# Attention block on one core: 12 of 72 probability units of a pass are turned by VectorE and transfers in place of TensorE

## The reference

```python
y = x * rsqrt(mean(x * x) + 1e-6) * rms_w           # x: 2 x 1024 x 512
q, k, v = split(y @ w_in.T)                          # 32 q heads, 8 k heads, 8 v heads, 64 wide
qk = rope(q) @ rope(k).T * 64 ** -0.5, causal
o = softmax(qk) @ v
x = layernorm(x + (x + o @ w_out.T))
x = layernorm(x + ternary(x) @ (ternary(weight) + variation).T)
```

## Time and profile before

| | |
|---|---|
| median of 3 runs | 1429.83 us (1427.52 to 1430.16) |
| the profiled execution | 1428.65 us, its span 1426.9 us |
| TensorE busy | 1355.1 us, 95% |
| VectorE busy | 1148.0 us, 80% |
| ScalarE busy | 1077.9 us, 76% |
| GpSimd busy | 872.0 us, 61% |
| granted TensorE clock | 0.988 of full |
| moved by transfers | 61.79 MB |

### The profile page before, as it was taken

How to read it: one execution, slowest core, us unless ns; L and a number is a source line. 1 busy time by engine, 2 the same in 40 slices (tenths; PEclk the granted TensorE clock), 3 DMA queues, 4 the chain that set the end, 5 groups by cost and what they waited for, 6 DMA issues and landing times.

```text
span 1426.9 us, 25073 instructions
## 1 busy us (share of the span) xinstructions
PE 1355.1 (95%) x7296; PEld 1112.1 (78%) x7296; DVE 1148.0 (80%) x3031; ACT 1077.9 (76%) x2277; POOL 872.0 (61%) x846
## 2 busy tenths in 40 slices
PE   4799999999999999999999999999999999997787
PEld 3678787888888888888888888888888888885565
DVE  5687777888787888888797888888797887876897
ACT  4768778787787878778787878778787878785553
POOL 1457467476646766376656766376646766477766
PEclk9799999999999999999999999999999999998999
DMA  6002101211101111111101111111101111111012
GB/s 206 20 19 60 49 26 28 54 30 45 35 24 49 55 29 31 50 34 46 34 24 49 55 29 31 44 40 45 34 24 49 51 33 31 29 37 51 31 46 77
DMA packets 45160, 61.79 MB, mean 43 GB/s; under 512 B 10464, under 2 KB 27104, under 8 KB 45024
## 3 DMA queue, kind: packets, MB, share of 16 engines
q1 hardware_dynamic: 45024, 60.20, 14.6%
HBM read 34.74 MB, written 4.46 MB: 27 GB/s over the span
## 4 chain that ended last, share of the span: by engine, by line
PE 74%; DVE 9%; ACT 6%; issue 4%; POOL 3%; DMA 3%; SPq 1%; DVEq 0%; POOLq 0%; ACTq 0%
PE s L1081 17%; PE x L1093 16%; PE t L1127 14%; PE x L1111 9%; PE ot L1052 8%; PE ot L1050 8%; DMA spread<-recip_rows 3%; DVE prob L949 2%; DVE prob_lo L1017 2%; ACT prob L781 2%; ACT prob_hi L752 1%; PE x L1101 1%; DVE win_lo L967 1%; DVE stats L843 1%; ACT q_t L816 1%
## 5 line engine op out<-in xcount | busy, mean ns | idle before, releaser
L752 ACT ACTIVATE prob_hi<-t 128x512 fp32r<-128x512 f32 x576 | 340.2, 594 | 150.7 <-PE t L1127 144.4
L1017 DVE TENSOR_TENSOR prob_lo<-t,prob_hi 128x512 fp32r<-128x512 f32 x576 | 394.4, 686 | 64.0 <-ACT prob_hi L752 58.1
L1081 PE MATMUL s<-k_t,q_t 128*128 128x512 f32 (+3 forms) x1536 | 411.1, 372 | 24.7 <-DVE neg_max L949 13.7
L781 ACT ACTIVATE prob<-prob,neg_max 128x896 f32<-128x896 f32 (+7 forms) x512 | 393.3, 770 | 36.6 <-DVE neg_max L949 35.1
L1127 PE MATMUL t<-ident,prob 128*128 128x128 f32 x2304 | 348.1, 274 | 2.8 <-ACT prob L781 2.7
L1127 PEld LDWEIGHTS t<-ident,prob 128*128 128x128 f32 x2304 | 288.7, 141 | 77.6 <-ACT prob L781 4.9
L949 DVE CUSTOM_DVE_ANT_0 prob<-s,mask 128x512 f32<-128x512 f32 (+3 forms) x512 | 292.3, 585 | 62.8 <-PE s L1081 38.9
L1081 PEld LDWEIGHTS s<-k_t,q_t 128*128 128x128 f32 x1536 | 246.0, 192 | 60.7 <-DVE neg_max L949 19.8
L725 POOL TENSOR_TENSOR o_lo<-o_raw,o_hi 128x256 fp32r<-128x256 f32 x128 | 95.0, 742 | 256.5 <-ACT o_hi L836 255.9
L1050 PE MATMUL ot<-prob_hi,v_sb 128*128 128x512 f32 x576 | 239.9, 416 | 3.8 <-DVE o_raw L999 3.0
L1052 PE MATMUL ot<-prob_lo,v_sb 128*128 128x512 f32 x576 | 232.8, 404 | 8.3 <-DVE prob_lo L1017 8.3
(11 more groups left out here) (88 smaller groups left out, 2051.7 us busy)
## 6 DMA issues: line engine op xcount, KB each, us to landing
swapped<-flat SPq DMA_DIRECT2D x320, 64.0 KB, 2.0
spread<-recip_rows SPq DMA_DIRECT2D x128, 128.0 KB
recip_rows<-turned SPq DMA_DIRECT2D x512, 0.5 KB
raw<-L_attn_w_in SPq DMA_DIRECT2D x8, 768.0 KB, 7.7
raw<-L_attn_w_out SPq DMA_DIRECT2D x8, 512.0 KB, 3.7
out<-acc SPq DMA_DIRECT2D x16, 256.0 KB, 2.0
acc<-L_attn_x SPq DMA_DIRECT2D x3, 1024.0 KB, 10.1
acc<-L_attn_x SPq DMA_DIRECT2D x4, 256.0 KB, 3.6
```

The source lines that it names most:

```text
L752: act.activation(prob_hi[:, u % 2, :], t_ps[u % 2][:, :], ACT.Copy).then_inc(prob_hi_done, 1)
L781: act.activation(row, row, ACT.Exp, bias=neg_max[:, kk % 4, h:h + 1], scale=-1.0, accum_out=total[:, kk % 4, h:h + 1]).then_inc(ex_done, 1)
L1017: dve.tensor_tensor(prob_lo[:, u % 2, :], t_ps[u % 2][:, :], prob_hi[:, u % 2, :].bitcast(F32), ALU.subtract).then_inc(prob_lo_done, 1)
L1081: mm = pe.matmul(s_ps[:, off:off + cols], q_t[:, h, s * P:(s + 1) * P], k_t[:, part, keys:keys + cols], start=(part == 0), stop=(part == 1))
```

## The change

Six units of each batch, (s, j) = (5,3), (6,3), (6,4), (7,3), (7,4), (7,5), twelve of 72 in a pass and 96 in the program, no longer go through TensorE's transposes and PSUM. Instead:

1. `bt` on VectorE: one transpose instruction, in place, turns the 16 pieces of 32x32 of the unit's 128x512 block.
2. `bt` on SP: one transfer of 256 KB takes the block to `block_rows` in memory (four slots).
3. `bm` on SP: four transfers of 64 KB bring it back, so that each piece lands on its own partitions.
4. ScalarE's `prob_hi` and VectorE's `prob_lo` read these units from `prob` in SBUF.

For this the rows are laid out anew, for all units: within a unit's 512 columns the head is the innermost index, so a head's consecutive keys lie four floats (16 bytes) apart. VectorE's score write, ScalarE's exponential (read and write) and TensorE's load of the block to be turned all use this step. A unit is now one slot of `prob`. `P_AFTER` and `P_BASE` stay. All tables of places are set anew, in all passes. The transposes of TensorE that stay are counted by `turns(u)`.

```diff
+BY_BLOCKS = ((5, 3), (6, 3), (6, 4), (7, 3), (7, 4), (7, 5))
+BLOCK_SLOTS = 4
...
+    for n, (made, moved) in enumerate(at_pass["BLOCKS"]):
+        put(made, ("bt", n))
+        put(moved, ("bm", n))
...
+        def blocks_before(u):
+            return sum(b * UNITS + first_unit(s) + j < u for b, s, j in map(block_unit, range(AWAY)))
+        def by_blocks(u):
+            return u < BODY and unit_of(u)[1:] in BY_BLOCKS
+        def turns(u):
+            passes, u = divmod(u, BODY)
+            return passes * (BODY - AWAY) + u - blocks_before(u)
...
-            start, cols = P_BASE[s] * BANK, (s + 1) * P
-            return prob[:, start + h * cols:start + (h + 1) * cols]
+            start, cols = (P_BASE[s] + 4 * c) * BANK, min(HALF, s + 1 - 4 * c) * BANK
+            return prob[:, start:start + cols].rearrange("p (k h) -> p h k", h=HG)[:, h]
...
SP:
+                        elif e[0] == "bt":
+                            wait(sp, blocks_done, g, AWAY, n + 1)
+                            wait(sp, blocks_in[some], g, 64 * ROUNDS, 64 * (n // BLOCK_SLOTS))
+                            sp.dma_start(block_d[some], prob_unit(*block_unit(n)[1:])).then_inc(blocks_out[some], 16)
+                        elif e[0] == "bm":
+                            wait(sp, blocks_out[some], g, 16 * ROUNDS, 16 * (n // BLOCK_SLOTS + 1))
+                            from_d = block_d[some].rearrange("(a j) (b f) -> b j a f", a=4, b=4)
+                            to = prob_unit(*block_unit(n)[1:]).rearrange("p (a f) -> p a f", a=4)
+                            for b in range(4):
+                                sp.dma_start(to[32 * b:32 * b + 32], from_d[b]).then_inc(blocks_in[some], 16)
ScalarE:
+                        if by_blocks(u):
+                            wait(act, blocks_in[n % BLOCK_SLOTS], g, 64 * ROUNDS, 64 * (n // BLOCK_SLOTS + 1))
+                            act.activation(hi.rearrange("p (h q) -> p h q", h=HG),
+                                           prob_unit(s, j).rearrange("p (q h) -> p h q", h=HG), ACT.Copy)
VectorE:
+                        elif e[0] == "bt":
+                            wait(dve, ex_done, g, 2 * NT * HG, (b * NT + s + 1) * HG)
+                            cells = prob_unit(s, j).rearrange("p (b i h) -> p b h i", b=4, h=HG)
+                            dve.transpose(cells, cells).then_inc(blocks_done, 1)
...
+                        if by_blocks(u):
+                            dve.tensor_tensor(lo, prob_unit(s, j).rearrange("p (q h) -> p h q", h=HG), hi, ALU.subtract)
TensorE:
+                        if not by_blocks(u):
+                            for h in range(HG):
+                                cells = prob_unit(s, j).rearrange("p (k h) -> p h k", h=HG)[:, h]
+                                mm = pe.transpose(t_ps[u % 2][:, h * P:(h + 1) * P], cells, ident[:, :])
```

More of the change, by code:

```diff
@@ L96 @@
     SCORES=(
[14 rows of a table removed]
[14 rows of a table added]
     ),
     PROJECT=(
[5 rows of a table removed]
[5 rows of a table added]
     ),
-    SQUARES=(0, 3),
+    SQUARES=(2, 39),
     NORMS=(
-        (20, 24), (26, 34), (36, 41), (42, 44), (49, 57), (65, 97), (107, 136), (151, 167)
+        (9, 21), (22, 27), (39, 46), (47, 56), (59, 62), (65, 113), (125, 143), (149, 160)
     ),
-    W_OUT=(10, 20),
-    LOAD=213,
-    W_IN=(296, 296, 300, 300),
+    W_OUT=(12, 38),
+    LOAD=221,
+    W_IN=(262, 263, 283, 284),
     OUTPUT=(
[3 rows of a table removed]
[3 rows of a table added]
+    ),
+    BLOCKS=(
+        (111, 128), (153, 175), (158, 178), (192, 227), (195, 240), (234, 240), (402, 409), (437, 454), (437, 468),
+        (508, 517), (510, 524), (511, 537)
     ))
@@ L133 @@
     SCORES=(
[14 rows of a table removed]
[14 rows of a table added]
     ),
     PROJECT=(
[4 rows of a table removed]
-    ),
-    W_OUT=(51, 51),
-    LOAD=177,
-    W_IN=(255, 260, 287, 294),
[4 rows of a table added]
+    ),
+    W_OUT=(49, 57),
+    LOAD=196,
+    W_IN=(261, 287, 297, 302),
     OUTPUT=(
[3 rows of a table removed]
[3 rows of a table added]
+    ),
+    BLOCKS=(
+        (113, 117), (150, 189), (155, 190), (200, 220), (203, 228), (218, 252), (402, 412), (445, 457), (456, 467),
+        (493, 523), (497, 524), (502, 526)
     ))
@@ L265, in first_plan, with seq_block @@
     return plan.number()
-def seq_block(nc, x, w_in, w_out, rms_w, ffn_w, ffn_r, cos, sin, ident_d, tri_d, row_d, out):
+def seq_block(nc, x, w_in, w_out, rms_w, ffn_w, ffn_r, cos, sin, ident_d, tri_d, row_d, block_d, out):
     B, S, D = x.shape
@@ L390, in seq_block @@
         t_done = sem("t_done")
+        blocks_done = sem("blocks_done")
+        blocks_out = [sem(f"blocks_out{n}") for n in range(BLOCK_SLOTS)]
+        blocks_in = [sem(f"blocks_in{n}") for n in range(BLOCK_SLOTS)]
         recip_done = sem("recip_done")
@@ L474, in unit_of, with block_unit @@
             return b, s, u - first_unit(s)
+        AWAY = 2 * len(BY_BLOCKS)
+        def block_unit(n):
+            b, n = divmod(n, len(BY_BLOCKS))
+            return b, *BY_BLOCKS[n]
+        def blocks_before(u):
[5 more added lines that the diff above has]
+            return passes * (BODY - AWAY) + u - blocks_before(u)
+        TURNS = BODY - AWAY
+        ROUNDS = AWAY // BLOCK_SLOTS
         def over_bodies(eng, one):
@@ L489, in xn_tile, with prob_row, prob_unit @@
             return scratch(9 + t % 3) if t < FIRST_TILES else raw[:, 2, :]
-        def prob_row(s, h):
-            start, cols = P_BASE[s] * BANK, (s + 1) * P
-            return prob[:, start + h * cols:start + (h + 1) * cols]
+        def prob_row(s, h, c):
+            start, cols = (P_BASE[s] + 4 * c) * BANK, min(HALF, s + 1 - 4 * c) * BANK
+            return prob[:, start:start + cols].rearrange("p (k h) -> p h k", h=HG)[:, h]
+        def prob_unit(s, j):
+            return prob[:, (P_BASE[s] + j) * BANK:(P_BASE[s] + j + 1) * BANK]
         def below(eng, t):
@@ L748, in one @@
                     if u < plan.units:
-                        wait(act, t_done, g, BODY, u + 1)
                         wait(act, pv_done, g, BODY, u - 1)
-                        act.activation(prob_hi[:, u % 2, :], t_ps[u % 2][:, :], ACT.Copy).then_inc(prob_hi_done, 1)
+                        hi = prob_hi[:, u % 2, :]
+                        if by_blocks(u):
+                            n, (_, s, j) = blocks_before(u), unit_of(u)
+                            wait(act, blocks_in[n % BLOCK_SLOTS], g, 64 * ROUNDS, 64 * (n // BLOCK_SLOTS + 1))
+                            act.activation(hi.rearrange("p (h q) -> p h q", h=HG),
+                                           prob_unit(s, j).rearrange("p (q h) -> p h q", h=HG), ACT.Copy
+                                           ).then_inc(prob_hi_done, 1)
+                        else:
+                            wait(act, t_done, g, TURNS, turns(u) + 1)
+                            act.activation(hi, t_ps[u % 2][:, :], ACT.Copy).then_inc(prob_hi_done, 1)
                     for e in plan.ahead[u] + plan.behind[u]:
@@ L776, in one @@
                             kk = b * NT + s
-                            row = prob_row(s, h)
                             wait(act, max_done, g, STEPS_MADE, scored(b, s, h, s // HALF) + 1)
                             wait(act, recip_done, g, 2 * NT, kk - 3)
+                            start = P_BASE[s] * BANK
+                            row = prob[:, start:start + (s + 1) * BANK].rearrange("p (k h) -> p h k", h=HG)[:, h]
                             act.activation(row, row, ACT.Exp, bias=neg_max[:, kk % 4, h:h + 1], scale=-1.0,
@@ L943, in events @@
                             back, last = P_AFTER[s]
-                            wait(dve, t_done, g, BODY, (b + back) * UNITS + first_unit(last + 1))
+                            wait(dve, t_done, g, TURNS, turns((b + back) * UNITS + first_unit(last + 1)))
                             wait(dve, sc_full, g, STEPS_MADE, n + 1)
@@ L948, in events @@
                                 wait(dve, max_done, g, STEPS_MADE, n - 1)
-                            dve.tensor_tensor_reduce(out=prob_row(s, h)[:, c * BANK:c * BANK + cols],
+                            dve.tensor_tensor_reduce(out=prob_row(s, h, c),
                                                      in0=s_ps[:, off:off + cols], in1=mask[:, seen:seen + cols],
@@ L1016, in one @@
                         wait(dve, pv_done, g, BODY, u - 1)
-                        dve.tensor_tensor(prob_lo[:, u % 2, :], t_ps[u % 2][:, :], prob_hi[:, u % 2, :].bitcast(F32),
-                                          ALU.subtract).then_inc(prob_lo_done, 1)
+                        hi, lo = prob_hi[:, u % 2, :].bitcast(F32), prob_lo[:, u % 2, :]
+                        if by_blocks(u):
+                            _, s, j = unit_of(u)
+                            hi, lo = [x.rearrange("p (h q) -> p h q", h=HG) for x in (hi, lo)]
+                            dve.tensor_tensor(lo, prob_unit(s, j).rearrange("p (q h) -> p h q", h=HG), hi, ALU.subtract
```

(14 more changed lines are left out.)

18 lines of the change are left out of this document (14 added, 4 removed), and 147 rows, old and new, of tables (FIRST, LAYER, OUTPUT, PROJECT).

## The result

The changed kernel takes 1791.93 us (median of 4 runs, 1791.05 to 1794.64), beside 1429.99 of the kernel before: a ratio of 1.254 (95% interval 1.2524 to 1.2554), 362 us more. The forecast of 1413 us is wrong, and the time lies beyond the range's upper end of 1600.

A forecast was written before the change was run, and what follows sets the result against it. TensorE was taken to bound the six middle passes. Seven passes at 5.3 - 2.5 us saved, rounded to -19.6, and +2.6 in the final pass gave -17 us: 1411.6, or 1413 in the runs' terms; range 1388 to 1600.

The forecast's parts named there:

- The layout: ... I take nothing: VectorE's write, ScalarE's exponential and TensorE's load at the 16-byte step: taken as no extra cost, one element a cycle.
- the turning point: VectorE's columns at the 16-byte step: over 0.38 ns extra each, from 14 us of room over 36,864 columns, decides for slower.
- the text's upper bound of a doubled column: 16-byte step, a column costing twice: per pass VectorE 38 us plus 13, ScalarE 31 us, TensorE 26 us.
- Rival 1: The 16-byte step costs: 1461 if only ScalarE pays, about 1600 if TensorE, 1690 or more if VectorE; chance 0.31.
- +2.5 us a pass for tables: All places dealt anew: TensorE idles 2.5 us more a pass, half of what was freed; bounds 0 and 5.3.
- VectorE still has 14 us: Said against rival 2 (VectorE or transfers eat the gain, 1422 to 1450, chance 0.17): VectorE keeps 14 us of room.
- TensorE removed: TensorE's transposes of 12 units gone: 12 x 0.44 = 5.3 us a pass, 42 us in eight passes at most.
- Transpose 0.71 us: VectorE's in-place transpose of a 512-column unit: 0.71 us, 8.5 us a pass; bounds 0.46 and 3.4 us.
- Low part +0.15 us: VectorE's low part with both inputs in SBUF: 0.15 us more a unit, 1.8 us a pass; bounds 0 and +1.07.
- VectorE's work lies in its room: VectorE a pass: 132.8 + 8.5 + 1.8 = 143 us of about 157, 91% where it was 82%.
- Transfers at nothing: SP's store and four loads a unit: 35 us a pass on SP, costed at nothing; without cover 36 us a pass.
- ScalarE's high part 619 ns: ScalarE's high part read from SBUF: 619 in place of 594 ns, 0.3 us a pass, nothing on the path.

The follow-up runs named there:

- third kernel of its group: Kernel before with its places, keys innermost, TensorE's 12 turns a pass gone, no transfers, no VectorE transposes, low part from PSUM (other output): 1410.1 us, ratio 0.9869.
- 1434.2: Kernel before with its places, keys innermost, 12 blocks a pass turned by VectorE, no transfers, low part from a PSUM bank (other output): 1434.2 us, ratio 1.0037.
- the kernel of 1475.8: Changed kernel with rows as before, turned blocks in runs of 32 floats, new tables, all block transfers left out (other output): 1475.8 us, ratio 1.0324.
- the first kernel: Kernel before with its places, keys innermost, 12 blocks a pass turned by VectorE, no transfers, low part from SBUF (other output): 1463.4 us, ratio 1.0241.
- the kernel with eight transfers a block: Changed kernel with rows as before, turned blocks in runs of 32 floats, four stores in 128-byte pieces and four loads a block: 1604.2 us, ratio 1.1226.

## Why the prediction was wrong

**The step that failed** is "The layout: ... I take nothing". The sum needed a price for an access no row had, and took the lower bound because engines with very different access run at a column a cycle. But all those rows walk neighbouring floats on the SBUF side, and so said nothing on it. Measured, each engine pays: VectorE's write 1082 - 685 = 397 ns for 512 columns, 0.78 ns a column, twice the 0.38 ns at which the text itself put the turning point; ScalarE 1011 ns for 1024, 0.99 a column. For ScalarE that is over the text's upper bound of a doubled column (0.84 ns more). By the step alone the kernel loses 207 us, by the step in the whole change 296. The Trainium skill, page Advanced Engine Details and Errata, section SBUF Cachelines, gives the rule that the text named and set aside: a 16-byte line has to be hit twice, or the access pays. The runs agree with it for VectorE and nearly for ScalarE: two floats of 16 bytes are free or almost, one is not. For TensorE's load the measurement differs: 202 ns with two, 206 with one.

**Rival 1**, with 0.31, is what happened in kind. Its sizes were near for work, low for time: VectorE 194 us a pass against 173 measured, ScalarE 160 against 172, "1690 or more" against 1792. But the rival reckoned with one full engine, and VectorE isn't full in the middle passes; it is 83% busy. What the runs show is that two engines' longer pieces both count (110 us went with ScalarE's, 90 stayed with VectorE's), and that no engine is full: with a pass of 207 us, VectorE still stands idle 34 us. That the pass became a chain through engines that wait for each other is read from the waits above and fits both; no run tests it by itself. TensorE's part was far too high, 26 us a pass from a doubled load; the runs give 7 to 11 us in eight passes.

**The sum's other terms, without the step.** The text foresaw +2.5 us a pass for tables and "VectorE still has 14 us". Measured from the kernel before to the change without the step:

| part | us | from |
|---|---|---|
| TensorE's turns gone | -19 | third kernel of its group less 1429 |
| transposes on VectorE | +24 | 1434.2 - 1410.1 |
| low part from SBUF | +29 | 1463.4 - 1434.2 |
| new tables (rows in runs of 32) | +12 | 1475.8 - 1463.4 |
| transfers | +20 | 1495.8 - 1475.8 |
| the step | +296 | 1791.9 - 1495.8 |

The first three and the last are differences of one edit (the first also gives each unit one slot of `prob`, floats side by side). The two rows between are not: the kernel of 1475.8 has rows in runs of 32 and its neighbours have not, so only their sum, 32 us for tables and transfers (1495.8 - 1463.4), is one. All sizes hold in this order alone, since the parts meet: the tables cost 38 us with the old work, and the transfers 2 in the changed kernel. Added from the other end, with the step first, the same 362 us are 207 for the step, 35 for the tables, 119 for the blocks and 2 for the transfers. So by that order over a third of the 296 us in the last row is not the old work made dearer, but the blocks' own work done at the dear step.

- *TensorE removed*: the -19 lies near the -17 forecast in all, but by luck. The text took all 5.3 us a pass as coming back, less 2.5 for new tables under a fuller VectorE. Here the tables are the old ones and VectorE has nothing more to do, and still only 2.8 us a pass come back.
- *Transpose 0.71 us*: right, 0.697 without the step; with it 1.138.
- *Low part +0.15 us*: too small; 0.85 to 1.04 by kernel in place of 0.69 without the step, 1.24 with it. The bound had held it.
- *VectorE's work lies in its room*: wrong, and this would have turned the sign without the step: 96 transposes are 66 us of work and cost 24, 96 longer low parts add 30 us of work and cost 29. The room of 14 us a pass is a mean, and added work isn't spread evenly: between 640 and 660 us of the first kernel VectorE went from 16.4 us, no more than its mean, to 19.1. The low part costs its whole length, and TensorE does wait for it: in the pass from 600 to 764 us 2.9 us (5.1 its weight loads), where a pass of the kernel before (483.6 to 644.7 us) had 0.2 (0.7). Where the transposes' 24 us are paid, no trace shows.
- *Transfers at nothing*: right for the changed kernel (2 us). Wrong without the step, about +20, and very wrong for tables not made for them, +87 with six blocks.
- *ScalarE's high part 619 ns*: 627 without the step, 1127 with it.

The chances were badly set too: the step's cost got 0.31, although no row showed it free and a rule said that it isn't, and the range ended at 1600, below its worst case. The worst single-engine price in it, with "or more", already stood at 1690.

**Still open.** The granted clock fell to 0.95 in the changed kernel, and is 0.946 without its transfers. At 0.95 a tenth of the pass ran at the lower of TensorE's levels (1.2 GHz, half of full), so as an estimate at most 10 us of a pass of 207 are TensorE's from that. How much of it reaches the end, where TensorE is idle 28 us a pass, no run here separates. The same holds for the kernel with eight transfers a block (0.946, and 0.986 without them): part of its 128 us may be the clock's, and so may part of the six blocks' 87 us (0.96, and 0.983 without transfers) and of the 119 us of blocks beside the step (0.946, and 0.979 without blocks). No run has tables planned for the blocks with floats side by side.

## What to carry to other kernels

Before a layout is changed to make a transfer simple, price the new step on every engine that touches the tile; if no row has that step, the range has to reach the doubled column on all of them at once, and past what the fullest engine alone would need. Here the pass came to 185 us with the fullest engine at 164 (step alone) and to 207 with it at 173, well short of both engines' additions summed (46 us more for 83 us of added work). A mean of room over a pass doesn't tell whether added work is hidden: look at windows of a few units where it will fall, and at who waits for the operation that grows. Where one engine issues all transfers in order, as SP here, a transfer's price can be that of what stands behind its wait.

## What the runs showed of the hardware

- A step of 16 bytes between floats: VectorE's write of 128x512 685 to 1082 ns, transpose in place 697 to 1138, two-input subtraction 978 to 1237; ScalarE's exponential in place of 1024 columns 1148 to 2159, its read of 512 alone 627 to 1127. One of 8 bytes: VectorE 686, no loss; ScalarE 1241, 8% more; TensorE's load of 128 columns 202 ns, as at 16 bytes (206 and 207), where contiguous took 141.
- A column costs VectorE's write and ScalarE's exponential the same at 16 bytes, 1.82 ns, though they differ when contiguous (1.03 and 0.84).
- TensorE hides most of its longer load: in the changed kernel's chain, which the profile shows there from 1208 us, 7 of 12 groups of four turns up to 1300 us take 0.47 to 0.49 us, as with 8 bytes; the rest, 0.70 to 0.87. Part of the latter comes with contiguous loads too: the kernel with the step but contiguous loads has 0.44 at 15 places between 500 and 620 us and 0.66 at 4.
- Reading VectorE's accumulator takes 83 ns behind a contiguous write and 158 behind one of 16 bytes, though it writes one column.
- A VectorE subtraction with both inputs in SBUF takes between 0.65 and 1.79 us, mean 997 ns, in the kernel of old places; with PSUM as one input it takes 686 (684 for the same twelve units).
